# Pre-norm causal attention and feed-forward layer on one core: value matmuls two steps behind the scores, three probability buffers

## The reference, cut to what matters

```python
xn = layernorm(x)
Q, K, V = xn @ Wq.T, xn @ Wk.T, xn @ Wv.T        # 16 heads of 16
Q, K = rope(Q), rope(K)
scores = Q @ K.T / sqrt(16)                       # 2048 x 2048 a head, keys after the query masked
x = x + (softmax(scores) @ V) @ Wo.T
x = x + relu(layernorm(x) @ w1 + b1) @ w2 + b2    # 256 -> 1024 -> 256
```

## Time and profile before

| | us |
|---|---|
| median of 3 runs (2079.06 to 2081.48) | 2079.61 |
| profiled execution | 2078.35 |
| its span, first to last instruction | 2076.6 |
| TensorE busy | 1935.3 (93%) |
| VectorE busy | 1861.4 (90%) |
| ScalarE busy | 1504.3 (72%) |
| GpSimd busy | 617.7 (30%) |

### The profile page before, as it was taken

The page is one execution under the profiler, slowest core; times in us unless marked ns, Lnnn a source line. Parts: engine busy times, 40 slices in busy tenths (PEclk is TensorE's granted clock), DMA queues, the critical chain, the costliest instruction groups (busy, mean ns, idle before and its releaser), DMA issues. The chain is left out here.

```text
span 2076.6 us, 53487 instructions
## 1 busy us (share of the span) xinstructions
PE 1935.3 (93%) x19104; PEld 777.1 (37%) x19104; DVE 1861.4 (90%) x3959; ACT 1504.3 (72%) x3252; POOL 617.7 (30%) x1249
## 2 busy tenths in 40 slices
PE   5886599999999999999999999999999879999998
PEld 3443122232222323223233232332223246777776
DVE  7997899999999999999999999999999057777775
ACT  6995088888888898888988889888888823333332
POOL 7998521121221212212022120221212323333331
PEclk9999599999999999999999999999999989999999
DMA  5678231330313303033030321303210212222220
GB/s 188 232 246 231 94 70 31 63 69 18 71 33 69 69 18 70 25 78 63 23 70 23 80 46 41 70 23 80 42 35 19 73 59 86 86 87 81 81 86 26
DMA packets 133319, 153.17 MB, mean 74 GB/s; under 512 B 23904, under 2 KB 99424, under 8 KB 132832
## 3 DMA queue, kind: packets, MB, share of 16 engines
q1 hardware_dynamic: 133088, 150.19, 27.9%
HBM read 90.38 MB, written 59.77 MB: 72 GB/s over the span
## 5 line engine op out<-in xcount | busy, mean ns | idle before, releaser
L912 ACT ACTIVATE s_prob<-s_ps 128x512 f32<-128x512 f32 (+3 forms) x2560 | 1198.4, 536 | 179.7 <-PE s_ps L755 147.6
L840 DVE TENSOR_REDUCE s_part<-s_ps 128x2 f32<-128x1024 f32 x768 | 875.8, 1214 | 8.3 <-PE s_ps L738 7.4
L774 PE MATMUL s_ps<-s_prob,s_v 128*32 128x256 f32 (+3 forms) x10240 | 737.4, 360 | 14.3 <-ACT s_o L903 11.6
L738 PE MATMUL s_ps<-mk,mq 64*128 64x512 f16 (+3 forms) x2560 | 680.3, 357 | 56.5 <-DVE s_part L840 21.1
L755 PE MATMUL s_ps<-aq,ak 64*128 64x512 f16 (+3 forms) x2560 | 715.9, 351 | 4.5 <-ACT s_prob L912 1.5
L942 POOL TENSOR_SCALAR_AFFINE_SELECT s_prob<-s_prob 128x128 f32<-128x128 f32 x1024 | 286.1, 293 | 1093.3 <-ACT s_prob L912 1080.5
L847 DVE CUSTOM_DVE_ANT_0 s_ps<-s_ps,mask_sb 128x512 f32<-128x512 f32 (+3 forms) x1024 | 462.7, 525 | 4.0 <-PE s_ps L738 3.1
L774 PEld LDWEIGHTS s_ps<-s_prob,s_v 128*32 128x32 f32 x10240 | 201.9, 108 | 433.5 <-issue 214.8
L755 PEld LDWEIGHTS s_ps<-aq,ak 64*128 64x128 f16 x2560 | 177.0, 93 | 489.3 <-ACT s_prob L912 459.0
L738 PEld LDWEIGHTS s_ps<-mk,mq 64*128 64x128 f16 x2560 | 166.6, 93 | 129.4 <-DVE s_part L840 51.3
L1210 ACT ACTIVATE s_h_f<-s_ps,s_b_s 128x512 f32<-128x512 f32 x128 | 88.0, 687 | 105.7 <-PE s_ps L1075 84.8
(11 more groups left out here) (98 smaller groups left out, 1615.8 us busy)
## 6 DMA issues: line engine op xcount, KB each, us to landing
v_scratch<-s_vst SPq DMA_DIRECT2D x32, 512.0 KB, 4.0
s_v<-v_scratch SPq DMA_DIRECT2D x16, 1024.0 KB, 10.7
att_scratch<-s_o SPq DMA_DIRECT2D x64, 256.0 KB, 2.4
aq<-qk_scratch SPq DMA_DIRECT2D x96, 128.0 KB, 4.4
ak<-qk_scratch SPq DMA_DIRECT2D x96, 128.0 KB, 6.9
s_xin<-x SPq DMA_DIRECT2D x16, 512.0 KB, 4.3
qk_scratch<-s_r_lo SPq DMA_DIRECT2D x64, 128.0 KB, 2.3
qk_scratch<-s_r_hi SPq DMA_DIRECT2D x64, 128.0 KB, 2.4
```

The lines of the kernel that those rows point to most:

```text
L738: nc.tensor.matmul(ps[:, bank_of(use + jj), 0:w], mq[rows, p, pair, qt * P:(qt + 1) * P], mk[rows, p, pair, kc * CH:kc * CH + w], start=Tr ...
L774: last = nc.tensor.matmul(ps[32 * j:32 * j + 32, O_BANK, cols], v[:, p, kb, j, :], prob[:, s % 2, j, cols], start=kb == 0 and part == 0, s ...
L840: nc.vector.tensor_reduce(part[:, qt // TPC, :, pair, qt % TPC, kc], ps[:, bank_of(use):bank_of(use) + 2, 0:w], AX.X, ALU.max).then_inc(m_ ...
L912: nc.scalar.activation(prob[:, s % 2, j, q0:CH], ps[:, s_bank(s, j), q0:CH], ACT.Exp, scale=1.0 / (SQK * DK ** 0.5)).then_inc(p_done, 1)
```

## The change

- The value matmuls run two steps behind the scores instead of one (`BEHIND = 2`), with three probability buffers instead of two (`NPROB = 3`, `prob_of`). After the last step of the last iteration, the value matmuls of two steps are left to do.
- The order of the full steps (couples of one score and one max matmul) is now used in all steps that have max tiles, the masked ones too. `max_pair` makes head 1 first, waits for each head's bank on its own, and VectorE reads head 1 first in masked steps.
- The output copy stands behind the third exponential (`COPY_HEAD = 2`) of the second step after a chunk's last one, instead of behind the fourth exponential of the first step after it.
- SyncE loads the rows of chunk 1 before it stores the output of the previous iteration's last chunk.

```diff
+        NPROB = 3
-        prob = sb("s2_prob", [P, 2, G, CH], F32)
+        prob = sb("s2_prob", [P, NPROB, G, CH], F32)
+        BEHIND = NPROB - 1
+        COPY_HEAD = G - 2
+        def prob_of(i, s):
+            return prob[:, (NS * i + s) % NPROB]
...
                 store_rows(i, 1)
+                load_rows(i, 1)
                 if not first:
                     store(i - 1, NC - 1)
-                load_rows(i, 1)
...
-            def max_pair(t, pair, heads=(0, 1)):
+            def max_pair(t, pair, heads=(1, 0)):
...
-                    if crosses_diagonal(qt, kc):
-                        pe.wait_ge(m_read, use + jj + 1)
-                    elif jj == heads[0]:
-                        pe.wait_ge(m_read, use + 2)
+                    pe.wait_ge(m_read, use + 2 - jj)
...
             def value_step(i, p, s, part):
-                if s > 0:
-                    pv_step(i, p, s - 1, part)
+                if s >= BEHIND:
+                    pv_step(i, p, s - BEHIND, part)
                 elif i > 0:
-                    pv_step(i - 1, 1 - p, NS - 1, part)
+                    pv_step(i - 1, 1 - p, NS + s - BEHIND, part)
...
-                    if t < STEPS_M and not is_diagonal(s):
+                    if t < STEPS_M:
...
-                    if t < STEPS_M:
-                        max_pair(t, 0)
-                    elif is_diagonal(s):
+                    if is_diagonal(s):
                         filler_pair(p, s, 0)
...
-            pv_step(NIT - 1, 1, NS - 1, 0)
-            pv_step(NIT - 1, 1, NS - 1, 1)
+            for s in range(NS - BEHIND, NS):
+                for part in range(2):
+                    pv_step(NIT - 1, 1, s, part)
...
-                for jj in range(2):
+                for jj in (1, 0):
                     bank = bank_of(use + jj)
-                    dve.wait_ge(m_ready, use + jj + 1)
+                    dve.wait_ge(m_ready, use + 2 - jj)
...
             def copy_o(i, c):
-                act.wait_ge(pv_done, NS * i + CHUNK_END[c] + 1 + 2)
+                act.wait_ge(pv_done, NS * i + CHUNK_END[c] + 1 + NPROB)
...
-                    if s == 0 and not first:
-                        copy_o(i - 1, NC - 1)
-                    for cc in range(NC):
-                        if cc != LATE and s == CHUNK_END[cc] + 1:
-                            copy_o(i, cc)
+                        if j == COPY_HEAD and s == BEHIND - 1 and not first:
+                            copy_o(i - 1, NC - 1)
+                        for cc in range(NC):
+                            if j == COPY_HEAD and cc != LATE and s == CHUNK_END[cc] + BEHIND:
+                                copy_o(i, cc)
...
-            pool.sem_inc(pv_done, 2)
+            pool.sem_inc(pv_done, NPROB)
```

More of the change, by code:

```diff
@@ L774, in pv_step @@
                     last = nc.tensor.matmul(ps[32 * j:32 * j + 32, O_BANK, cols], v[:, p, kb, j, :],
-                                            prob[:, s % 2, j, cols], start=kb == 0 and part == 0,
+                                            prob_of(i, s)[:, j, cols], start=kb == 0 and part == 0,
                                             stop=kb == TPC * (c + 1) - 1 and part == 1)
@@ L815, in iteration @@
                     score_tile(i, p, s, 3)
-                    if t < STEPS_M:
-                        max_pair(t, 1)
-                    elif is_diagonal(s):
+                    if is_diagonal(s):
                         filler_pair(p, s, 1)
@@ L911, in iteration @@
                         act.wait_ge(s_ready, ST * i + G * s + j + 1)
-                        nc.scalar.activation(prob[:, s % 2, j, q0:CH], ps[:, s_bank(s, j), q0:CH], ACT.Exp,
+                        nc.scalar.activation(prob_of(i, s)[:, j, q0:CH], ps[:, s_bank(s, j), q0:CH], ACT.Exp,
                                              scale=1.0 / (SQK * DK ** 0.5)).then_inc(p_done, 1)
-                    if s == 0 and not first:
-                        copy_o(i - 1, NC - 1)
-                    for cc in range(NC):
-                        if cc != LATE and s == CHUNK_END[cc] + 1:
-                            copy_o(i, cc)
+                        if j == COPY_HEAD and s == BEHIND - 1 and not first:
[3 more added lines that the diff above has]
+                                copy_o(i, cc)
             act.sem_inc(p_done, G)
@@ L938, in mask_step @@
                 for j in range(G):
-                    block = prob[:, s % 2, j, q0:q0 + P]
+                    block = prob_of(i, s)[:, j, q0:q0 + P]
                     pool.wait_ge(p_done, ST * i + G * s + j + 1 + G)
```

## The result

| | before | after |
|---|---|---|
| median, 20 runs each | 2079.67 us | 2091.39 us |
| lowest to highest | 2078.29 to 2086.8 | 2078.61 to 2094.81 |
| ratio | | 1.0027, 95% interval 1.0015 to 1.004 |
| profiled execution | 2078.35 | 2082.8 |
| its span | 2076.6 | 2081.1 |

What follows compares the result with a forecast made beforehand. VectorE was taken as the bound, with TensorE held at the max banks. Terms -4.2 + 0.3 + 0.5 - 1.8 + 0.9 = -4.3 us on the profiled 2078.35 gave 2074.05, so a 2075.3 us forecast, range 2065 to 2083.

Steps and rivals of the forecast that it cites:

- 13 us are the most that can be had: Stage 2: VectorE's work sums to 1387 of 1400 us, so reordering saves at most some 13; its waits sum to 14.9.
- the 0.46 us of waiting at 546.01: VectorE ahead of step 12's first reduction: starts at 546.47 what it could have started at 546.01, in each iteration.
- The second rival: All of VectorE's waits go, the 0.46 us too: -13.6 + 0.9, 2066.9 us; chance 0.19.
- Wait at step 13 goes: -0.26 x 16: VectorE's 0.26 us wait at 550.12, behind the output copy, goes in each of 16 iterations: -4.2 us, bounds 0 and -4.5.
- So this wait stays: VectorE's wait behind step 11 goes from 0.46 to 0.47 us: +0.3 us in all, bounds -5 to +2.4.
- cover the same lateness: At the other three chunk changes of an iteration, VectorE's chunk end of 0.84 us hides TensorE's lateness.
- Copy at steps 1 and 2, +0.5: Copy ends about 0.07 us after the value part wants to start; part reaches VectorE in step 3: +0.5 us (0 to +1.2).
- Iteration 0, -1.8: First four steps of iteration 0, at 1.2 GHz: TensorE's shorter work wins back -1.8 us of 3.4 lost.
- The end, +0.9: End of the last iteration: one more step of value matmuls is left, less a copy stall: +0.9 us (0 to +1.5).
- my first rival: Nothing to be seen: VectorE's beat is fixed and the 0.26 comes back in small waits; 2079 us, within 2; chance 0.25.
- Worth nothing of its own: A value matmul no longer waiting for the last exponential or GpSimd's select gains nothing by itself.
- The rival at 2090.9: The copy between third and fourth exponential stalls ScalarE at all 63 chunk changes: +12.2 us, total 2090.9; chance 0.13.

Runs made afterwards that it cites:

- the changed kernel with the fillers: Changed kernel plus filler matmuls in steps 24 to 26 of the last iteration: 2080.86 us, ratio 1.0003 to the kernel before.
- the old order and fillers: Kernel before plus the same filler matmuls in steps 24 to 26 of the last iteration: 2079.99 us, ratio 0.9992 to the kernel before.

## Why the prediction was wrong

**VectorE bounds, its beat is fixed, 13 us are the most that can be had.** Right. The beat is 1.131 us in after, and no version gained more than 3.3 us by its ratio. But the 0.46 us of waiting at 546.01 count 0.14 us of work: at 546.01 VectorE still had its accumulator to read, and the row itself says 0.33 us of idle time. Sixteen times that is 2 us that were never to be had, and the sum of 14.9 is nearer to 13. (The second rival's -13.6 is -13.3 by the terms given.)

**Wait at step 13 goes: -0.26 x 16.** Right: VectorE's step 13 takes 2.263 us (median over the iterations) against 2.514, so -0.25. The two steps behind alone (without the couples in masked steps) have it too, 2.263; the couples alone don't, 2.513; and with the copy behind the fourth exponential it is 2.262. So the extra step does it, and the copy's place among the exponentials, on which the walk spent its 0.1 us of margin, doesn't matter.

**"So this wait stays", +0.3, and the other chunk ends "cover the same lateness".** This is the failed step of the sum: -3.4 us for the loop, where nothing came. I compared VectorE's 40 steps in before and in the changed kernel with the fillers, whose trace has no fall there, by their medians over the iterations. Exactly five differ by over 0.003 us: step 13 by -0.251, step 11 by +0.107, and steps 3, 23 and 39, the other three ends of a chunk, by +0.053, +0.050 and +0.054. The sum is +0.013 us: what was gained at one place came back at four, in small waits. Where they come from shows in a masked step of 128 columns, first before, then after with the fillers:

```profile
528.31 0.33 DVE L847 CUSTOM_DVE_ANT_0 s_ps<-s_ps,mask_sb 128x128 f32<-128x128 f32 x1
528.56 0.33 DVE L847 CUSTOM_DVE_ANT_0 s_ps<-s_ps,mask_sb 128x128 f32<-128x128 f32 x1
```

```profile
526.90 0.33 DVE L847 CUSTOM_DVE_ANT_0 s_ps<-s_ps,mask_sb 128x128 f32<-128x128 f32 x1
527.23 0.30 DVE L847 CUSTOM_DVE_ANT_0 s_ps<-s_ps,mask_sb 128x128 f32<-128x128 f32 x1
```

Second to third reduction: 0.25 us apart before, 0.33 after. The second pair's tile stands behind a value part of 192 columns where 128 stood. I had priced the wider value matmuls by step and found them paid by the couples; inside the step they are late for the second pair. The kernel with two steps behind alone, which has the wider matmuls and no couples, fits: the same four steps are 0.13 to 0.20 us longer than before. That makes +1.7 us for step 11 and +2.5 for the three others, against -4.0.

**Copy at steps 1 and 2, +0.5.** It is within the +0.053 of step 3. That ScalarE shows waits inside the steps that hold a copy, which I had named as a sign of being wrong, came, with 0.57 us and no price.

**Iteration 0, -1.8.** Right in direction, near in size by this pair of traces: VectorE's first four steps take 9.94 us (257.84 to 267.78) against 11.41, so -1.5. But iteration 0 differs by as much between executions of one program: 88.26 to 89.26 us in the four traces of the changed kernel, 89.28 with the old order and fillers and 90.54 in before. The pair with fillers gives -1.0.

```profile
257.84 0.70 DVE L847 CUSTOM_DVE_ANT_0 s_ps<-s_ps,mask_sb 128x512 f32<-128x512 f32 x1
...
267.78 1.23 DVE L840 TENSOR_REDUCE s_part<-s_ps 128x2 f32<-128x1024 f32 x1 [0.22 <-PE s_ps L741]
```

**The end, +0.9.** Right where the clock holds: 44.06 against 43.24 us from step 20 to the last value matmul, +0.82. SyncE at nothing: nothing on the path showed it.

With these sizes, 0 in the loop, -1.5 and +0.8, the sum is -0.7: about 2079 us, the time of my first rival and its mechanism, waits that come back. The two traces with fillers, where no clock falls, agree: 1399.8 against 1400.6 us from the first score to the last value matmul, -0.7.

**The clock.** This is the other failed step, a term that the prediction put at nothing. The rest, from 2079 to the median of 2091.4 in the first measurement (2080.6 to 2085.2 in the other three), goes with the falls: 1.3 to 1.4 us for each short one behind step 1, 9 to 11.5 for a long one at the end. The prediction used the clock for iteration 0 and took the earlier trace rows's 1.00 as given for the rest, though it moved value matmuls of 64 columns to tiles of 384. The 256 columns that stood there before were worth nothing to VectorE's beat, but with them the trace of before shows no fall in the loop. The Trainium skill, "TensorE: Matmul & The Clock Gate", A second HAM failure mode: psum-queue depth-cycling, says that small idle times between groups of matmuls, coming often, are enough to make the clock go back and forth. The traces agree so far as the fall needs no long idle time: ahead of 1311.7 TensorE's longest is 0.15 us, and it is busy 3.12 of 3.40 us by modelled ends. Whether it is such gaps or the thin matmuls themselves that bring the fall, no run here tells.

**"Worth nothing of its own".** I said so of a value matmul that needn't wait for the select. True in the old order, and false with the couples, which make it a wait of 0.34 to 0.41 us in eight of an iteration's sixteen masked steps: either half of the change alone costs some 30 us.

**The rival at 2090.9** has nearly the measured median by chance: its mechanism, the copy, is refuted by the run with the copy behind the fourth exponential, and by the iterations without a fall, which lose nothing.

## What to carry to other kernels

Where another engine sets the pace, TensorE's surplus work isn't only cost: before matmuls are moved, add up what each step keeps after the move, and see that two thin things don't meet. When long executions of one program go with a low mean clock, list the stretches of low clock one by one, since slices of 50 us don't show them; filling the thin stretch with matmuls whose results nobody needs is a test and a remedy in one (here it cost 0.07 us an iteration). A gain of 0.25 us at one wait is to be compared with the same engine's whole loop, step by step: four small waits took it back.

## What the runs showed of the hardware that wasn't expected

- TensorE's granted clock goes to 0.50, its 1.2 GHz level, behind a stretch in which the engine was never idle for long (3.12 us busy of 3.40). A fall lasts 3.41 or 6.83 us in the loop and costs an iteration of the changed kernel 1.3 to 1.4 us with 3.41.
- At the end of stage 2, around steps 25 and 26 of the last iteration, a fall lasts 3.4, 6.8, 17 or 24 to 31 us, or doesn't come, by kernel and execution. In the long ones the clock stays down although TensorE is busy throughout (53.99 of 56 us by the profile).
- Whether falls come, and how many, differs between executions of one program, and in a trace they often repeat at the distance of one lengthened iteration, 88.75 us. Why is open.
